# Two small LayerNorm operations on VectorE instead of GpSimd, in a fused decoder layer

## What is computed

```python
def _layernorm(x, axis=-1, eps=1e-05):
    m = jnp.mean(x, axis=axis, keepdims=True)
    v = jnp.var(x, axis=axis, keepdims=True)
    return (x - m) / jnp.sqrt(v + eps)

def reference(x, ctx_1024, ...):
    x = x + _L0_attn_ref(_layernorm(x), Wq, bq, Wk, bk, Wv, bv, Wo, bo)
    x = x + _L0_xattn_ref(_layernorm(x), ctx_1024, ctx_1024, Wq, bq, ...)
    x = x + _L0_ffn_ref(_layernorm(x), weight, aux_weight1, aux_weight2, bias)
    return x
```

## Time and profile before

| | us |
|---|---|
| median of 3 runs | 2504.38 |
| lowest and highest | 2502.93, 2504.84 |
| profiled execution | 2503.5 |
| its span | 2501.8 |
| PE busy in it | 2335.8 |
| DVE busy | 1700.1 |
| ACT busy | 1384.2 |
| POOL busy | 717.8 |

### The profile page before, as it was taken

The page is one execution under the profiler, slowest core; times in us unless marked ns, Lnnn a source line. Parts: engine busy times, 40 slices in busy tenths (PEclk is TensorE's granted clock), DMA queues, the critical chain, the costliest instruction groups (busy, mean ns, idle before and its releaser), DMA issues.

```text
span 2501.8 us, 67273 instructions
## 1 busy us (share of the span) xinstructions
PE 2335.8 (93%) x22072; PEld 1856.7 (74%) x22072; DVE 1700.1 (68%) x3710; ACT 1384.2 (55%) x3066; POOL 717.8 (29%) x1371
## 2 busy tenths in 40 slices
PE   4799999999999999999999999999999999999995
PEld 3677777777777777777777777777777777777763
DVE  4477667767767767767767767776776776776752
ACT  2455555565565555555555555556556556556551
POOL 3132233233233233233222223223223323323321
PEclk9899999999999999999999999999999999999995
DMA  8333433443343343333343343344344334334320
GB/s 157 88 101 96 110 97 85 107 112 86 104 112 83 101 106 93 105 103 85 101 107 93 101 107 93 89 107 104 90 107 105 85 100 113 92 100 109 86 69 21
DMA packets 167370, 244.83 MB, mean 98 GB/s; under 512 B 22176, under 2 KB 90512, under 8 KB 164248
## 3 DMA queue, kind: packets, MB, share of 16 engines
q1 hardware_dynamic: 165660, 244.22, 37.4%
q10 hardware_dynamic: 1664, 0.01, 0.1%
HBM read 53.13 MB, written 33.56 MB: 35 GB/s over the span
## 4 chain that ended last, share of the span: by engine, by line
PE 53%; DVE 11%; DMA 10%; issue 9%; ACT 8%; POOL 4%; SPq 4%; ACTq 0%; DVEq 0%; POOLq 0%
PE ps_misc L540 14%; PE ps_score L614 7%; PE ps_misc L526 6%; PE ps_attend L639 5%; DMA k_stack<-k_nat 5%; DMA q_stack<-neg_max_t_s 5%; DVE neg_max_s L954 4%; PE ps_misc L669 4%; PE ps_misc L510 3%; PE ps_score L615 3%; PE ps_max L597 3%; ACT xprobs L804 3%; PE ps_score L624 2%; DVE chain_t L937 2%; PE ps_attend L643 2%
## 5 line engine op out<-in xcount | busy, mean ns | idle before, releaser
L797 ACT ACTIVATE probs<-ps_score 128x384 f32<-128x384 f32 x1024 | 468.6, 494 | 113.3 <-PE ps_score L615 111.1
L954 DVE TENSOR_REDUCE neg_max_s<-ps_max 128x2 f32<-128x512 f32 (+1 forms) x768 | 478.7, 678 | 8.4 <-PE ps_max L585 4.4
L804 ACT ACTIVATE xprobs<-ps_score 120x512 f32<-120x512 f32 x512 | 280.7, 603 | 222.9 <-PE ps_score L624 222.8
L1080 POOL TENSOR_SCALAR ve_LN<-mv_LN 128x2 f32<-128x2 f32 x192 | 36.8, 191 | 1213.6 <-DVE mv_LN L976 1213.6
L614 PE MATMUL ps_score<-q_stack,k_stack 128*128 128x256 f32 x1024 | 353.2, 351 | 27.6 <-DMA q_stack<-neg_max_t_s 13.9
L962 DVE TENSOR_REDUCE neg_max_x<-ps_max 128x4 f32<-128x480 f32 x512 | 313.8, 649 | 61.1 <-PE ps_max L597 61.1
L615 PE MATMUL ps_score<-q_stack,k_stack 128*128 128x256 f32 x1024 | 283.8, 281 | 0.0
L614 PEld LDWEIGHTS ps_score<-q_stack,k_stack 128*128 128x128 f32 x1024 | 193.9, 189 | 109.3 <-ACT probs L797 47.1
L624 PE MATMUL ps_score<-xq_stack,xk_stack 128*120 128x256 f32 x1024 | 228.6, 316 | 6.6 <-DMA xq_stack<-neg_max_t_x 2.8
L1106 POOL TENSOR_TENSOR res<-res,chain_n 128x512 f32<-128x512 f32 x64 | 82.5, 1288 | 442.9 <-ACT chain_n L842 442.9
L597 PE MATMUL ps_max<-xk_stack,xq_stack 127*128 127x120 bf16 x2048 | 195.3, 220 | 1.2 <-DVE neg_max_x L962 1.2
(11 more groups left out here) (147 smaller groups left out, 5365.2 us busy)
## 6 DMA issues: line engine op xcount, KB each, us to landing
k_stack<-k_nat SPq DMA_DIRECT2D x192, 256.0 KB, 3.6
q_stack<-q_nat SPq DMA_DIRECT2D x192, 256.0 KB, 3.7
xq_stack<-q_nat SPq DMA_DIRECT2D x192, 256.0 KB, 3.6
xk_stack<-scr_xk SPq DMA_DIRECT2D x192, 128.0 KB, 2.9
x_in<-in_x SPq DMA_DIRECT2D x64, 256.0 KB, 2.8
scr_xk<-k_nat SPq DMA_DIRECT2D x32, 512.0 KB, 3.4
out_y<-res SPq DMA_DIRECT2D x64, 256.0 KB, 2.2
ctx_in<-in_ctx SPq DMA_DIRECT2D x32, 240.0 KB, 4.1
```

What stands on the lines that cost most here:

```text
L797: act.activation(probs[:, h % 8, :], bank_of("SCORE", i, b, h)[:, P:4 * P], ACT.Exp)\
L804: act.activation(xprobs[0:C, at:at + 2, :], blocks(bank_of("XSCORE", i, b, u))[0:C], ACT.Exp).then_inc(sem("xprobs_ready"), 1)
L954: dve.tensor_reduce(o, ins, AX.X, ALU.max, negate=True).then_inc(sem("max_taken"), 1)
```

## The change

Variance plus epsilon and the negated mean are computed on DVE, right behind the aggregation and a wait for it, for all three LayerNorms. POOL then has two small operations left of four: the power, and negated mean times rstd, which gives `nmr` directly. The semaphore that releases POOL is raised by the second new operation.

```diff
             def moments(kind, src, ready):
-                st, mv = ln_sb[kind][0:2]
+                st, mv, ve, nmean = ln_sb[kind][0:4]
...
                     for a in range(NB):
-                        last = dve.bn_aggr(mv[:, a, :], st[:, a, :])
-                    last.then_inc(sem(f"{kind}_moments"), 1)
+                        dve.bn_aggr(mv[:, a, :], st[:, a, :]).then_inc(sem(f"{kind}_aggregates"), 1)
+                    wait(dve, f"{kind}_aggregates", 2, i, b, 2)
+                    alone(dve)
+                    dve.tensor_scalar(ve[:, :].unsqueeze(2), mv[:, :, 1:2], EPS, None, ALU.add)
+                    dve.tensor_scalar(nmean[:, :].unsqueeze(2), mv[:, :, 0:1], -1.0, None, ALU.mult)\
+                        .then_inc(sem(f"{kind}_moments"), 1)
...
             def normalise(kind, src, dst, free, bias_name, biased):
 
-                st, mv, ve, rstd, mr, nmr = ln_sb[kind]
+                ve, nmean, rstd, nmr = ln_sb[kind][2:6]
 
                 def f(i, b, _):
                     wait(pool, f"{kind}_moments", 1, i, b, 1)
                     alone(pool)
                     s = f"{kind}_small"
-                    pool.tensor_scalar(ve[:, :].unsqueeze(2), mv[:, :, 1:2], 1.0, EPS, ALU.mult, ALU.add)\
-                        .then_inc(sem(s), 1)
-                    wait(pool, s, 4, i, b, 1)
                     pool.tensor_tensor(rstd[:, :], ve[:, :], half[:, :], ALU.pow).then_inc(sem(s), 1)
-                    wait(pool, s, 4, i, b, 2)
-                    pool.tensor_tensor(mr[:, :].unsqueeze(2), mv[:, :, 0:1], rstd[:, :].unsqueeze(2), ALU.mult)\
-                        .then_inc(sem(s), 1)
-                    wait(pool, s, 4, i, b, 3)
-                    alone(pool)
-                    pool.tensor_scalar(nmr[:, :], mr[:, :], -1.0, 0.0, ALU.mult, ALU.add).then_inc(sem(s), 1)
-                    wait(pool, s, 4, i, b, 4)
+                    wait(pool, s, 2, i, b, 1)
+                    pool.tensor_tensor(nmr[:, :], nmean[:, :], rstd[:, :], ALU.mult).then_inc(sem(s), 1)
+                    wait(pool, s, 2, i, b, 2)
                     free(i, b)
```

More of the change, by code:

```diff
@@ L216, in build @@
         ln_sb = {n: (sb(f"st_{n}", [P, NB, 6]), sb(f"mv_{n}", [P, NB, 2]), sb(f"ve_{n}", [P, NB]),
-                     sb(f"rstd_{n}", [P, NB]), sb(f"mr_{n}", [P, NB]), sb(f"nmr_{n}", [P, NB]))
+                     sb(f"nmean_{n}", [P, NB]), sb(f"rstd_{n}", [P, NB]), sb(f"nmr_{n}", [P, NB]))
                  for n in ("LN1", "LN2", "LN3")}
```

## The result

| | before | after |
|---|---|---|
| median, us (13 runs each) | 2504.28 | 2498.87 |
| lowest and highest | 2501.98, 2506.34 | 2495.34, 2501.32 |
| profiled execution | 2503.5 | 2500.8 |
| its span | 2501.8 | 2498.9 |

The ratio is 0.9979, with a 95% interval of 0.9971 to 0.9988: the kernel got 5.4 us faster (3.0 to 7.3), just over the 0.2% that a measurement can tell. The forecast was 2506, no change or slightly slower. The time lies in the range, at its lower end, but on the other side of no change.

A forecast was written before the change was run, and what follows sets the result against it. The prediction took TensorE, busy 93%, as the bound, so only work it waits for counts. Per pair 0.13 + 0.15 - 0.18 = +0.10 us, +3.1 in 31 pairs, less 1.4 at the ends: +1.7 on 2504.4, 2506 us, range 2498 to 2516.

The forecast's parts named there:

- both prices: Per LayerNorm, VectorE is held 0.39 us by the new operations and wait; GpSimd's normalised tile comes 0.28 us earlier.
- LN3 and LN1: LN3's transpose gains 0.18 us per pair, in the even step; VectorE's hold at LN1 and LN3 costs nothing.
- MAX 9: TensorE's matmul in LN2's stretch that waits for a VectorE reduce: 0.31 us later in even steps, 0.15 in odd.
- LN2 in A, +0.13: LN2 in the even step: held maxima make TensorE and ScalarE later, +0.13 us, ends 0 and 0.39.
- MAX_T: Transpose of the maxima, even step: held the full 0.39 us, hidden by ScalarE's order with 0.13 to spare.
- LN2 in B, +0.15: LN2 in the odd step: ScalarE is the last to arrive, so +0.15 us, ends 0 and 0.39.
- The sum: +0.10 us per pair of steps, +3.1 in 31 pairs, -1.4 for filling and draining, together +1.7 us.
- -1.4 at the ends: Filling and draining of the pipeline: five exposed LayerNorms gain 1.4 us, an estimate, ends 0 and -2.
- second branch of rival 2: TensorE gets from MAX 9 to LN2's transpose faster than thought, then takes GpSimd's gain; within rival 2's chance of 0.11.
- rival 2: Faster: the added wait on VectorE is free, hold 0.24 us, LN2 costs 0; 2497 us, chance 0.11.
- Rival 1: Slower: LN2's maxima become the gate (2518 us), or only LN3's gain is missing (2512); chance 0.32.

The follow-up runs named there:

- ln3_only: The change in LN3 alone, LN1 and LN2 left as in the kernel before; 2503.16 against 2506.13 us, ratio 0.9981.
- after_held: The changed kernel plus one more wait and two more unread small operations on VectorE behind LN2; 2523.63 us, ratio to before 1.0075.
- pool_pair: Kernel before, nothing moved to VectorE: GpSimd computes variance plus epsilon and negated mean back to back, one wait less; 2489.69 against 2503.25 us, ratio 0.9943.

## Why the prediction was wrong

- **Right: both prices.** The hold is 0.39, the tile 0.28 to 0.29 earlier, the pair of operations takes 0.24. The wait for its own semaphore left DVE idle for 0.15 us or slightly more (23.1 us in 148 waits). The Trainium skill, page VectorE: DVE Perf Modes, section "The DRAIN you can't avoid", says that semaphores between the operations of a chain cost nothing extra; the trace does not agree at this wait either.
- **Right: LN3 and LN1.** LN3_T in A gained 0.18 and DVE's hold was covered there; `ln3_only` shows it by itself, and in the draining PE's waits for POOL fell from 1.06, 4.23 and 5.11 us to 0.79, 3.86 and 4.83, and one of 0.33 went.
- **Right: MAX 9.** It went 0.33 and 0.15 later, forecast 0.31 and 0.15. In A the matmul row has the bracket for DVE; in B only the row of the weight load has it (0.20).
- **Wrong: LN2 in A, +0.13.** The failed step is "PE then reaches LN2_T 0.31 later, having waited 0.17 for POOL there: +0.14". PE had waited 0.32, so a shift of 0.31 is covered. The idle time in a matmul's bracket runs from the modelled end of the matmul ahead, and matmuls overlap, so it is too short. ACT's 0.18 was misread in the same way: its copy starts 0.69 us behind LN2_T in both steps of before (1026.22 - 1025.53, 1064.38 - 1063.69) and 0.69 and 0.70 in after. It follows PE, and the stretch from exponential 6 to the copy shrank to 0.95 us in both steps of after, from 1.27 and 1.09. Measured: +0.02 at LN2_T.
- **Slightly wrong: MAX_T.** It was held 0.33 in A (3.95 us behind the aggregation before, 4.28 after), not 0.39, and ACT's order was to hide this "with 0.13 to spare". In fact a little came through. The copy of the maxima starts 1028.47 - 1027.24 = 1.23 us behind LN2_T, before 1026.71 - 1025.53 = 1.18, and SCORE 0 stands 1031.31 - 1027.24 = 4.07 behind LN2_T, before 4.01. ACT's rows of after:

```profile
1027.93 0.62 ACT L782 ACTIVATE chain_t<-ps_misc 128x512 fp32r<-128x512 f32 x1
1028.47 0.27 ACT L836 ACTIVATE neg_max_t_s<-ps_misc 32x128 fp32r<-32x128 f32 x1
```

- **Wrong: LN2 in B, +0.15.** The failed step is "Here ACT is the last to arrive". The three waits per pair of the earlier trace rows, which the prediction itself counted as "LN2_T in both", said that POOL was. A matmul row without a bracket was taken for a row without a wait, while the weight load beside it had 0.20. PE had waited 0.15, all of the shift of MAX 9. Measured: 0.00.
- **The sum.** Forecast 0.13 + 0.15 - 0.18 = +0.10 per pair, measured -0.107: -0.18 + 0.02 at LN2_T and 0.03 twice behind SCORE 0, -0.10. The two terms of LN2 make +0.28 of which 0.08 was real, and 31 pairs of 0.21 are 6.4 us, nearly the whole miss of 7.1. With the true waits of 0.32 and 0.15 the prediction's own sum would have had nothing for LN2: -0.18 per pair and -1.4 at the ends, 2497.4.
- **Rivals.** The wait was not free, but the second branch of rival 2 is what happened: PE gets from MAX 9 to LN2_T in 2.16, where before it took 2.47 (A) and 2.30 (B). It had been given too little weight. Its time, 2497, was close by luck: it took LN3_T's 0.18 whole, of which 0.107 per pair is left, and 0.43 instead of 0.28 for each exposed LN. That POOL's gain would be taken at LN2 too, as that branch says, did not happen. Rival 1 put its turning point at a hold of 0.45 us. `after_held`, with 0.78, bears out that there is one, and is slower by the full second 0.39; by the table of paths a hold costs time against before from 0.39 on.

What stays open: why 0.02 to 0.03 us per step is left of SCORE 0's delay, what takes back part of LN3_T's 0.18 in `ln3_only`, and the last 0.7 us between -4.7 and the measured -5.4, which is inside the interval. The 2.5 us by which the profiled execution of after is later in the filling was not pursued.

## What to carry to other kernels

To find how long an engine really waited at a step, take the distance from start to start and compare it with the same distance where nothing is late. A matmul's bracket was too short here (0.17 for 0.32, none for 0.15), and that of its weight load too long (0.37 and 0.20); look at both rows. Ahead of a join, write the length of every path to it: a shortened path is worth only the distance to the next one, and work that is moved from one to the other can make them equal and the gain nothing. Look first for a shorter chain on the engine that has it: here two independent small operations issued back to back gave about three times what moving two of them gave.

## What the hardware showed unexpectedly

- A TENSOR_SCALAR of 128x256 on POOL with two per-partition operands takes 555 ns with multiply and add, 1223 ns with subtract and multiply, 1222 ns with multiply and subtract. One subtraction made the kernel 3.75% slower.
- On POOL a second small operation behind an independent first one starts 0.28 us after it, and the power behind both starts 0.15 after the second (`pool_pair`), where a dependent chain took 0.28, 0.78 and 0.39 from start to start. So the added independent operation put the power back by only 0.15 us, and the chain from ve to the tile still came out shorter, 1.71 us in A and 1.61 in B against 1.86 and 1.85.
